# Another fixed order of two streams' steps on four engines, in a two-stream transformer decoder

## The chip, the cores and the metric

The kernel runs on one core of one Trainium2 chip. A core has four compute engines that run their own instruction lists and meet only through semaphores: TensorE (PE; its weight loads are shown as PEld), ScalarE (ACT), VectorE (DVE) and GpSimd (POOL). SyncE (SP) issues the DMA transfers. The metric is the device time of one execution in microseconds (us); the median of several is compared.

## The reference

Input `x` and context `ctx` are 32 sequences of 64 tokens with 128 channels, float32. Six sub-layers follow one another; after each one, x becomes layernorm(x + sub-layer(x)). They are:

```
x = LN(x + causal self-attention with rope(x))           16 heads of 8
x = LN(x + cross-attention(x, ctx), per-head layer norm of q and k)
x = LN(x + FP4-quantised gated FFN(x))                   inner width 352
x = LN(x + linear-attention block with convolutions and MLP(x))
x = LN(x + causal cross-attention(x, ctx))
x = LN(x + mixture of 8 experts, top 2(x))               inner width 256
```

All 8 experts are computed for every token, and weighted with the router's top-2 shares.

## The kernel before

**Streams and passes.** A chunk is 512 tokens (8 sequences, 4 tiles of 128 tokens). Two chunks are worked on at once, as two streams, called A and B here; each has its own SBUF buffers and its own 4 of the 8 PSUM banks. Two passes of a loop cover the four chunks. Both passes run the same instructions. A pass ends when all four engines are through; SP then clears the semaphores and opens the next one.

**Who does what.** On each engine a generator `network(h)` yields between steps. A step is a wait or two and then one to some thirty instructions. `weave` interleaves the steps of both streams by a list written out by hand, so many steps of A, then so many of B, and so on:

```
def weave(first, second, order):
    turns = (first, second)
    for k, count in enumerate(order):
        for _ in range(count):
            next(turns[k % 2], None)
```

`ORDER` has one list for each of the four engines. An engine executes its list strictly in this order: a step whose semaphore isn't there holds everything behind it, of both streams. Within one stream the order of steps is that of the generators.

**The steps of an attention tile t** (three attention stages, 4 tiles each), with the short names that are used below:

- S (PE, L504, in the causal stages after the mask matmuls of L497): scores. S of tile t waits for Z of tile t-1, since there is one pair of score banks per stream.
- X (DVE, L1134): row maximum; Z (DVE, L1139): subtract it. E (ACT, L913): exp.
- T (PE, L485), twice per tile: turn one half of the probabilities. ACT copies each half out of the one bank that all of them use (C, L893), so each T waits for the C of the T before it.
- M (PE, L548): probabilities times values. R (DVE, L1149 and L1152): divide. H (PE, L535): turn the heads; ACT copies them (L904 or L906). P (PE, L516): output projection. H and P of a tile share bank 3 with M, so they wait for each other's readers.
- U (DVE, L1104): add the residual, then bn_stats (L1107) and bn_aggr (L1110). POOL adds eps (L1522) and takes the power -0.5 (L1525). N (DVE, L1115): normalise. U of a tile waits for N of the tile two before.

**Between the self- and the cross-attention** each stream normalises k and then q by head on DVE (L1204 to L1234: a sum, a mean, a difference; ACT squares, L876; a second sum, L1215; then three Newton steps of three small instructions, L1190 to L1196, and a product, L1234). PE turns the result (L573), ACT applies the gain (L883) and spreads q or two of four k copies (L863, L870); POOL spreads the other two (L1553) and adds the bias to the residual (L1542). PE computes A's q (L559) and its values (L471), and ACT copies the values (L853).

**The experts' stage.** For each of 16 halves g(n) (PE, L803, gate and up matmuls) goes to ACT's silu (L1037), then DVE's product h(n) (L1469); g(n) waits for h(n-1). For each of 8 experts o(e) (PE, L794) goes to four additions on DVE (L1461); o(e) waits for h(2e+1). Ahead of it stand the router (L782), the shares (DVE, L1419 to L1452), their turning (L810) and the bias product (L816).

## Time and profile before

| what | value |
|---|---|
| median of 3 runs | 825.92 us (825.36 to 827.03) |
| the profiled execution | 826.34 us |
| its span, first to last instruction | 824.5 us |
| around the span | 1.84 us |
| mean granted TensorE clock | 0.866 |
| instructions | 13333 |

The first pass's work on PE, ACT, DVE and POOL starts at 8.6 us and ends at 415.6 us of the span; the second starts at 417.4 us and ends at 821.8 us. The second repeats the first at a distance of about 406.3 us, so the readings below are of the first pass, and each difference counts twice. A granted clock of 1.00 is 2.4 GHz, one of 0.50 is 1.2 GHz.

### The profile page before, as it was taken

How to read it: one execution, taken by the hardware profiler on the slowest of the kernel's cores; microseconds unless marked ns; L12 is line 12 of the kernel's file. 1: busy time of each engine (PE TensorE's matmuls, PEld its weight loads, DVE VectorE, ACT ScalarE, POOL GpSimd, SP SyncE). 2: the span in 40 equal slices, each digit the busy share in tenths (PEclk: the TensorE clock that was granted, in tenths of full speed). 3: DMA queues.
4: the chain of work that ended last, by engine and by line, in shares of the span. 5: the costliest groups of instructions: out<-in, count | busy, mean ns of one | idle time of the engine just before them, and what ended most of it. 6: DMA issues, size and time to landing. Idle time of an engine off the chain costs nothing.

```text
span 824.5 us, 13333 instructions
## 1 busy us (share of the span) xinstructions
PE 651.3 (79%) x5090; PEld 428.0 (52%) x5090; DVE 558.4 (68%) x1482; ACT 334.7 (41%) x546; POOL 136.7 (17%) x258
## 2 busy tenths in 40 slices
PE   5886587666796987999878756967678969789995
PEld 3565456443553554566555644654345436546663
DVE  7868576897676744655648775788967667555445
ACT  2753363223845543222146443632156546332220
POOL 3313102111025020000131240020110430100002
PEclk9997577696999888999979965976869989789998
DMA  8101000000000000000000000000000000000000
GB/s 296 51 2 52 1 2 1 1 0 2 1 0 1 2 2 0 1 1 1 2 28 2 2 0 1 2 1 1 0 2 1 1 0 3 1 1 0 1 1 26
DMA packets 9011, 10.11 MB, mean 12 GB/s; under 512 B 1256, under 2 KB 7792, under 8 KB 8560
## 3 DMA queue, kind: packets, MB, share of 16 engines
q1 hardware_dynamic: 8944, 9.22, 3.4%
q8 instruction: 42, 0.69, 0.3%
q14 instruction: 25, 0.20, 0.1%
HBM read 8.17 MB, written 1.05 MB: 11 GB/s over the span
## 4 chain that ended last, share of the span: by engine, by line
PE 55%; DVE 26%; ACT 10%; issue 4%; POOL 3%; DMA 1%; SPq 1%; POOLq 0%; DVEq 0%; ACTq 0%
PE ps L803 14%; PE ps L794 7%; PE ps L485 5%; PE ps L504 5%; PE ps L548 3%; ACT s_probs L913 3%; DVE s_probs L1139 3%; DVE s_row_max L1134 3%; PE ps L471 2%; POOL s_rs L1525 2%; DVE s_x L1115 1%; DVE s_r L1104 1%; DVE s_st L1107 1%; PE ps L516 1%; DVE s_work L1080 1%
## 5 line engine op out<-in xcount | busy, mean ns | idle before, releaser
L1522 POOL TENSOR_TENSOR s_rs<-s_mv,eps 128x1 f32<-128x1 f32 x96 | 18.9, 199 | 547.7 <-DVE s_mv L1110 368.8
L1037 ACT ACTIVATE s_k<-ps,eb 128x512 f32<-128x512 f32 x64 | 44.0, 687 | 132.9 <-PE ps L803 132.8
L1469 DVE SCALAR_TENSOR_TENSOR s_pT<-ps,eb,s_k 128x512 f32<-128x512 f32 x64 | 48.0, 750 | 60.3 <-ACT s_k L1037 57.0
L1134 DVE TENSOR_REDUCE s_row_max<-ps 128x16 f32<-128x1024 f32 x48 | 58.6, 1222 | 40.9 <-PE ps L504 40.8
L485 PE MATMUL ps<-tabs,s_probs 128*128 128x128 f32 x384 | 67.2, 303 | 18.0 <-ACT s_probs L913 15.9
L893 ACT ACTIVATE s_pT<-ps 128x512 f32<-128x512 f32 x96 | 56.8, 594 | 46.1 <-PE ps L485 45.5
L803 PE MATMUL ps<-s_xT,wg 128*128 128x512 f32 x128 | 71.3, 641 | 1.5 <-DVE s_pT L1469 1.1
L794 PEld LDWEIGHTS ps<-wo,s_pT 128*128 128x128 f32 x512 | 61.7, 192 | 17.7 <-issue 12.4
L803 PE MATMUL ps<-s_xT,wu 128*128 128x512 f32 x128 | 68.5, 618 | 0.0
L504 PE MATMUL ps<-s_k,s_q 64*64 64x256 f32 x768 | 60.6, 439 | 9.2 <-ACT s_q L863 9.2
L485 PEld LDWEIGHTS ps<-tabs,s_probs 128*128 128x128 f32 x384 | 44.5, 150 | 41.3 <-ACT s_probs L913 24.8
L794 PE MATMUL ps<-wo,s_pT 128*128 128x128 f32 x512 | 63.0, 276 | 3.1 <-DVE s_pT L1469 3.1
L913 ACT ACTIVATE s_probs<-s_probs 128x1024 f32<-128x1024 f32 x48 | 50.4, 1053 | 26.8 <-DVE s_probs L1139 26.4
L1139 DVE TENSOR_TENSOR s_probs<-ps,s_row_max 128x1024 f32<-128x1024 f32 x48 | 58.7, 1223 | 1.5
L548 PEld LDWEIGHTS ps<-s_v,s_pT 128*64 128x64 f32 x1536 | 51.1, 144 | 12.2 <-issue 12.0
L548 PE MATMUL ps<-s_v,s_pT 128*64 128x18 f32 x1536 | 55.0, 216 | 2.3 <-ACT s_headsT L904 1.9
L1525 POOL TENSOR_TENSOR s_rs<-s_rs,minus_half 128x1 f32<-128x1 f32 x96 | 52.8, 551 | 7.2
L1553 POOL TENSOR_SCALAR s_k<-s_kT,tabs 128x512 f32<-128x512 f32 x24 | 38.3, 1607 | 44.6 <-DVE s_kT L1168 22.4
L1461 DVE SCALAR_TENSOR_TENSOR s_k<-ps,s_ew,s_k 128x128 f32<-128x128 f32 x128 | 36.0, 344 | 12.3 <-PE ps L794 12.3
L504 PEld LDWEIGHTS ps<-s_k,s_q 64*64 64x64 f32 x768 | 30.5, 153 | 25.4 <-ACT s_q L863 10.8
L803 PEld LDWEIGHTS ps<-s_xT,wu 128*128 128x128 f32 x128 | 25.9, 202 | 33.4 <-issue 33.4
L516 PE MATMUL ps<-mats,s_headsT 128*128 128x128 f32 x96 | 23.9, 339 | 15.8 <-DVE s_heads L1152 13.1
(223 smaller groups left out, 1157.3 us busy)
## 6 DMA issues: line engine op xcount, KB each, us to landing
s_cin<-in_ctx SPq DMA_DIRECT2D x4, 256.0 KB, 4.7
s_xin<-in_x SPq DMA_DIRECT2D x4, 256.0 KB, 5.1
wg<-in_wg SPq DMA_DIRECT2D x1, 1024.0 KB
wu<-in_wu SPq DMA_DIRECT2D x1, 1024.0 KB
wo<-in_wo SPq DMA_DIRECT2D x1, 1024.0 KB
out_x<-s_x SPq DMA_DIRECT2D x4, 256.0 KB, 2.5
mats<-in_mats SPq DMA_DIRECT2D x1, 832.0 KB, 6.4
fc<-in_fc SPq DMA_DIRECT2D x2, 256.0 KB, 5.5
```

What stands on the lines that cost most here:

```text
L485: ins = pe.transpose(h.ps[:, 2, tile(j)], h.probs[:, t % 2, 8 * part + 2 * j:8 * part + 2 * j + 2, :] .rearrange("p h k -> p (h k)"), ident)
L504: ins = pe.matmul(h.ps[S * b:S * b + S, half, 256 * side:256 * side + 256], h.q4[rows, side, S * sq:S * sq + S], h.k4[rows, sq, :, :].rear ...
L548: ins = pe.matmul(h.ps[S * b:S * b + S, 3, 18 * j:18 * j + 18], h.pT[:, t % 2, j, S * b:S * b + S], h.v2[:, 2 * t + b, 2 * j:2 * j + 2, :] ...
L794: ins = pe.matmul(h.ps[:, 2, tile(t)], h.ehid[:, e % 2, m, tile(t)], wo[:, 2 * e + m, :], start=m == 0, stop=m == 1)
L803: ins = pe.matmul(h.ps[:, k, 0:TOK], w[:, n // 2, P * (n % 2):P * (n % 2) + P], h.xT[:, :], start=True, stop=True)
L893: act.activation(h.pT[:, t % 2, 4 * part:4 * part + 4, :].rearrange("p j q -> p (j q)"), h.ps[:, 2, :], ACT.Copy).then_inc(h.pT_here, 1)
L913: act.activation(h.probs[:, u % 2, :, :], h.probs[:, u % 2, :, :], ACT.Exp).then_inc(h.exped, 1)
L1037: act.activation(h.esg[:, n % 2, :], h.ps[:, 0, 0:TOK], ACT.Silu, bias=eb[:, 0, n:n + 1]).then_inc(h.e_silu, 1)
L1134: dve.tensor_reduce(h.row_max[:, t % 2, :], s3, AX, ALU.max).then_inc(h.max_here, 1)
L1139: dve.tensor_tensor(h.probs[:, t % 2, :, :], s3, h.row_max[:, t % 2, :].rearrange("p (h o) -> p h o", o=1).to_broadcast([P, H, S]), ALU.su ...
L1469: dve.scalar_tensor_tensor(h.ehid[:, (n // 2) % 2, n % 2, :], h.ps[:, 1, 0:TOK], eb[:, 1, n:n + 1], h.esg[:, n % 2, :], ALU.add, ALU.mult) ...
L1525: pool.tensor_tensor(h.rs[:, t % 2:t % 2 + 1], h.rs[:, t % 2:t % 2 + 1], minus_half[:, 0:1], ALU.pow).then_inc(h.rstd_here, 1)
```

## The change

Only the order changes. The four lists of `ORDER` are replaced. Two places where the generators pause are changed too: `sum_norm` no longer pauses ahead of its wait on `x_new`, and `linear_block` pauses once per tile ahead of `sum_norm`. These two move no instruction within a stream; they change what one count in DVE's list means, and DVE has 614 steps where it had 642. The instructions, their operands and their waits are the same in number and kind.

```
 ORDER = {
     "pe": (
-        3, 3, 1, 1, 1, 1, 1, 1, 3, 3, 4, 2, 5, 2, 3, 1, 2, 1, 1, 2, 1, 1, 3, 4, 1, 1, 1, 4, 2, 3, 1, 2, 1,
...
+        1, 1, 2, 2, 1, 1, 2, 2, 3, 2, 1, 1, 2, 3, 2, 1, 4, 2, 3, 1, 2, 1, 1, 1, 5, 7, 1, 2, 2, 2, 1, 3, 1,
...
     "act": (
-        1, 1, 2, 2, 2, 1, 1, 2, 2, 1, 1, 1, 1, 1, 1, 1, 2, 1, 4, 2, 2, 1, 1, 2, 1, 4, 2, 1, 2, 2, 3, 3, 2,
...
+        3, 3, 3, 3, 2, 1, 1, 1, 2, 2, 1, 1, 2, 2, 3, 1, 1, 1, 2, 2, 3, 4, 3, 2, 2, 2, 2, 3, 3, 2, 2, 1, 1,
...
     "dve": (
-        1, 1, 4, 4, 2, 2, 2, 2, 4, 2, 4, 1, 2, 1, 7, 4, 3, 1, 4, 1, 1, 1, 3, 1, 1, 1, 5, 1, 2, 1, 4, 1, 3,
...
+        1, 1, 4, 4, 2, 2, 2, 2, 2, 1, 2, 3, 6, 2, 4, 2, 10, 1, 4, 1, 3, 1, 1, 2, 3, 1, 1, 2, 1, 1, 7, 3, 1,
...
     "pool": (
-        1, 1, 1, 1, 4, 1, 2, 2, 2, 1, 2, 6, 4, 2, 4, 6, 6, 2, 2, 2, 2, 6, 3, 2, 4, 1, 5, 9, 4, 2, 4, 6, 8,
-        8,),
+        1, 1, 1, 1, 4, 2, 1, 1, 4, 6, 1, 1, 8, 8, 4, 1, 4, 3, 2, 6, 2, 2, 10, 10, 5, 1, 3, 7, 4, 3, 1, 1,
+        1, 1, 1, 2, 1, 1,),
 }
@@ -1099,7 +1099,6 @@
                 n = sub * TILES + t + 1
                 if n >= 3:
-                    yield
                     dve.wait_ge(h.x_new, n - 2)
@@ -1386,6 +1385,7 @@
                     if u < TILES:
+                        yield
                         yield from sum_norm(h, 3, u, h.ps[:, 1, tile(u)], h.x[:, u, :])
```

Written out step by step, the two orders are alike in outline: in both, the streams go through the six stages almost in step, B a little behind A. They differ in the fine order within the stages. PE's steps in the self-attention (V: values, KQ: k of the next stage, QT: L573; the first digit of T is the tile, the second the half):

```
before AV BV AS0 BS0 AT0.0 AS1 AT0.1 BT0.0 BS1 BT0.1 AT1.0 AS2 AT1.1 AM0 BT1.0 BS2 AT2.0 AS3 AH0 AT2.1 AM1
       BT1.1 BM0 AP0 AT3.0 AH1 BT2.0 AT3.1 AM2 BS3 AP1 BH0 BT2.1 AH2 BM1 AM3 AKQ AP2 BP0 BT3.0 BH1 BT3.1 AH3
       BM2 AP3 BP1 BH2 BM3 BKQ AQT BP2 BH3 BP3 BQT
after  AV AS0 BV BS0 AT0.0 AS1 AT0.1 BT0.0 BS1 AT1.0 BT0.1 AS2 AT1.1 BT1.0 BS2 BT1.1 AM0 AT2.0 BM0 AS3 AH0
       AT2.1 AM1 BT2.0 BS3 AP0 AT3.0 AH1 BH0 AT3.1 AM2 BT2.1 AP1 BM1 AH2 AM3 AKQ AP2 AH3 BP0 BT3.0 BH1 BT3.1
       BM2 BP1 BH2 AP3 BM3 BKQ AQT BP2 BH3 BP3 BQT
```

In the causal cross-attention, from S2 of B on:

```
before BS2 AT2.0 AS3 AH0 AT2.1 AM1 BT1.1 BM0 AP0 AT3.0 AH1 BT2.0 AT3.1 AM2 BS3 AP1 BH0 AH2 BT2.1 BM1 AM3 ...
after  BS2 BT1.1 BM0 AT2.0 AS3 AH0 AT2.1 BT2.0 AM1 BS3 BH0 AP0 AT3.0 AH1 AT3.1 AM2 BT2.1 AP1 BM1 AH2 AM3 ...
```

At the start and the end of the experts' stage (r router, ew turned shares, bm bias product, tx x turned):

```
before Ag0 BM3 BP2 Ag1 BH3 BP3 Btx Aew Ag2 Br Bg0 Abm Ao0 Ag3 ... Bg11 Ag14 Ao6 Bg12 Ag15 Bo5 Bg13 Ao7 Bg14 Bo6 Bg15 Bo7
after  Ag0 BM3 BP2 BH3 BP3 Ag1 Btx Br Bg0 Aew Ag2 Abm Ao0 Ag3 ... Bg11 Ag14 Bg12 Bo5 Bg13 Ao6 Bg14 Ag15 Bo6 Bg15 Ao7 Bo7
```

Of the other engines these moves are spoken of below. ACT, at the start: before, B's q (L863) stands ahead of A's values (L853); after, A's values come first. DVE, self-attention: X3 and Z3 of B stand behind A's N0 before, and ahead of A's first bn_aggr after; R0 of B stands behind A's X3 and Z3 before, and ahead of them after. DVE, per-head norms: the second sum of A's q (L1215) stands behind B's last Newton steps and L1234 before, and ahead of B's last five Newton instructions, its U3, N2 and L1234 after. ACT, same place: B's L883 and L870 for k stand ahead of A's L883 for q in both, B's take of x behind it after. POOL: the power of B's tile 1 stands behind A's L1553 after, ahead of it before; A's L1542 stands behind B's tiles 2 and 3 and B's L1553 after, ahead of them before; in the linear block B's L1553 is moved behind A's norms and L1542. DVE and ACT, entry of the causal cross-attention: B's q (L1396) is moved between A's X0 and Z0, and ACT's spreading of it (L863) ahead of A's E0. DVE, FFN: A's last two tiles come up to 9 instructions later, B's up to 8 earlier. POOL and DVE, end of the pass: the final norms of A and B, one after the other before, alternate.

## Rows read from the trace of the kernel before

**Rows 1.** The page, part 1: busy time by engine, its share, instructions.

```profile
PE 651.3 (79%) x5090; PEld 428.0 (52%) x5090; DVE 558.4 (68%) x1482; ACT 334.7 (41%) x546; POOL 136.7 (17%) x258
```

**Rows 2.** Stretches of pass 1: length; busy us of PE, PEld, DVE, ACT, POOL; clock.

```profile
26.00:57.00 31.00, 26.57 (x424) 18.58 (x415) 23.55 (x34) 18.57 (x32) 3.69 (x6) 1.00 0.01 2
...
86.00:119.00 33.00, 24.73 (x240) 16.34 (x238) 19.89 (x31) 15.03 (x24) 0.53 (x1) 0.66 0.00 1
...
147.00:200.00 53.00, 33.01 (x128) 22.30 (x128) 46.71 (x149) 12.32 (x23) 8.71 (x21) 0.76 0.00 1
...
305.00:330.00 25.00, 20.80 (x103) 12.29 (x104) 10.94 (x54) 8.86 (x13) 2.24 (x6) 0.77 0.00 0
330.00:407.00 77.00, 75.72 (x349) 47.29 (x347) 43.79 (x131) 19.61 (x29) 2.54 (x8) 1.00 0.00 1
```

**Rows 3.** Timeline, self-attention, DVE: start, us; idle time before. B's X0, A's X3, B's X3.

```profile
29.77 1.23 DVE L1134 TENSOR_REDUCE s_row_max<-ps 128x16 f32<-128x1024 f32 x1 [0.25 <-PE ps L504]
...
43.99 1.21 DVE L1134 TENSOR_REDUCE s_row_max<-ps 128x16 f32<-128x1024 f32 x1
...
53.94 1.22 DVE L1134 TENSOR_REDUCE s_row_max<-ps 128x16 f32<-128x1024 f32 x1
```

**Rows 4.** Timeline, self- to cross-attention, ACT.

```profile
24.14 1.34 ACT L853 ACTIVATE s_v<-ps 64x256 f32<-64x256 f32 x4
...
77.90 1.36 ACT L853 ACTIVATE s_v<-ps 64x256 f32<-64x256 f32 x4 [4.82 <-PE ps L471]
79.28 0.63 ACT L876 ACTIVATE s_probs<-s_probs 128x512 f32<-128x512 f32 x1
```

**Rows 5.** Timeline, self- to cross-attention, POOL.

```profile
70.64 3.11 POOL L1553 TENSOR_SCALAR s_k<-s_kT,tabs 128x512 f32<-128x512 f32 x2 [3.85 <-ACT s_kT L883]
```

**Rows 6.** Timeline, self- to cross-attention, DVE.

```profile
73.83 1.20 DVE L1222 TENSOR_SCALAR s_work<-s_work 128x64 int32<-128x64 int32 x1
...
80.27 0.68 DVE L1215 TENSOR_REDUCE s_work<-s_probs 128x64 f32<-128x512 f32 x1
```

**Rows 7.** Timeline, first scores of the cross-attention, PE.

```profile
88.87 1.98 PE L504 MATMUL ps<-s_k,s_q 64*64 64x256 f32 x16 [2.29 <-ACT s_q L863]
```

**Rows 8.** Timeline, last norm of the FFN stage, DVE.

```profile
198.73 0.35 DVE L1115 TENSOR_SCALAR s_x<-s_r,s_mv,s_rs 128x128 f32<-128x128 f32 x1 [0.71 <-POOL s_rs L1525]
```

**Rows 9.** Timeline, entry of the causal cross-attention, ACT.

```profile
263.72 1.28 ACT L913 ACT_TABLE_LOAD   x1
```

**Rows 10.** Timeline, causal cross-attention, PE: M0 and S3 of B.

```profile
286.48 1.11 PE L548 MATMUL ps<-s_v,s_pT 128*64 128x18 f32 x32
...
291.54 1.03 PE L504 MATMUL ps<-s_k,s_q 64*64 64x256 f32 x16
```

**Rows 11.** Timeline, causal cross-attention, DVE: B's q; X3 of B; N3 of A.

```profile
264.99 0.74 DVE L1396 TENSOR_SCALAR s_qT<-ps,cols 128x512 f32<-128x512 f32 x1
...
294.01 1.22 DVE L1134 TENSOR_REDUCE s_row_max<-ps 128x16 f32<-128x1024 f32 x1
...
303.14 0.35 DVE L1115 TENSOR_SCALAR s_x<-s_r,s_mv,s_rs 128x128 f32<-128x128 f32 x1 [0.71 <-POOL s_rs L1525]
```

**Rows 12.** Timeline, start of the experts, PE: g1 of A, bias product, g5 of A.

```profile
312.68 1.58 PE L803 MATMUL ps<-s_xT,wg 128*128 128x512 f32 x2
...
326.94 1.15 PE L816 MATMUL ps<-bout,s_k 8*128 8x128 f32 x8
...
337.90 1.12 PE L803 MATMUL ps<-s_xT,wg 128*128 128x512 f32 x2 [0.56 <-DVE s_pT L1469]
```

**Rows 13.** Timeline, end of the pass, PE: o7 of B.

```profile
407.94 2.05 PE L794 MATMUL ps<-wo,s_pT 128*128 128x128 f32 x16 [1.56 <-DVE s_pT L1469]
```

**Rows 14.** Timeline, end of the pass, POOL: first and last norm of B.

```profile
411.65 0.19 POOL L1522 TENSOR_TENSOR s_rs<-s_mv,eps 128x1 f32<-128x1 f32 x1 [4.26 <-DVE s_mv L1493]
...
414.66 0.55 POOL L1525 TENSOR_TENSOR s_rs<-s_rs,minus_half 128x1 f32<-128x1 f32 x1
```

**Rows 15.** Timeline, end of the pass, DVE: last norm of B.

```profile
415.24 0.34 DVE L1115 TENSOR_SCALAR s_x<-s_k,s_mv,s_rs 128x128 f32<-128x128 f32 x1 [0.49 <-POOL s_rs L1525]
```

More of the change, by code:

```diff
@@ L93 @@
     "pe": (
[5 rows of a table removed]
-    "act": (
[5 rows of a table removed]
-    "dve": (
[8 rows of a table removed]
[5 rows of a table added]
+    "act": (
[4 rows of a table added]
+    "dve": (
[9 rows of a table added]
     "pool": (
-        1, 1, 1, 1, 4, 1, 2, 2, 2, 1, 2, 6, 4, 2, 4, 6, 6, 2, 2, 2, 2, 6, 3, 2, 4, 1, 5, 9, 4, 2, 4, 6, 8,
-        8,),
+        1, 1, 1, 1, 4, 2, 1, 1, 4, 6, 1, 1, 8, 8, 4, 1, 4, 3, 2, 6, 2, 2, 10, 10, 5, 1, 3, 7, 4, 3, 1, 1,
+        1, 1, 1, 2, 1, 1,),
 }
@@ L1101, in sum_norm @@
                 if n >= 3:
-                    yield
                     dve.wait_ge(h.x_new, n - 2)
@@ L1388, in linear_block @@
                     if u < TILES:
+                        yield
                         yield from sum_norm(h, 3, u, h.ps[:, 1, tile(u)], h.x[:, u, :])
```

36 rows, old and new, of the table ORDER are left out of this document.

## The prediction

> **What bounds the kernel now.** I read the page first. PE is busy for 79% of the span and DVE for 68% [rows 1], so neither is full, and an order can gain only where both wait. The change adds, removes and resizes nothing, so its price is all in waits. I therefore read the stretches next, for who is full where [rows 2]. From 330 to 407 us PE is busy for 75.72 of 77 us at the upper clock level (2.4 GHz): the experts can't shrink, only start earlier or end without holes. From 147 to 200 us DVE is busy for 46.71 of 53 us: the FFN's quantising is DVE's, and reordering can win a few us at most. In the attention stages nobody is full: in 26 to 57 us PE has 26.57 of 31 us and DVE 23.55. There the chain runs round DVE, ACT and PE, and each hole in DVE ahead of a row maximum shows in the timeline. These stages and their seams are where the fine order matters. The second pass repeats the first, so each difference counts twice.
>
> I then followed the new order of all four engines, stage by stage, with the durations of the timeline, and wrote down each time at which a step can start: the later of its data and of the step ahead of it on its engine. Six differences come out. Each is in us of one pass.
>
> **1. Self-attention and the seam behind it: +2.0.** The start moves one step. A's values are copied by ACT (1.34 us for the four parts [rows 4]) ahead of B's q, and A's first scores no longer wait for B's values on PE. That gives A 0.3 us, but B's copy chain starts 1.34 us later, and with it X0 of B (29.77 us, 0.25 us of idle time ahead of it [rows 3]) comes at 31.3 us: DVE idles. DVE's order makes A's next maximum wait for B's Z0, so A is late by 1.1 us from there. With 1.23 us for each X and Z [rows 3] DVE does X and Z of A1 from 33.7 us, of B1 from 36.9 us and of A2 from 39.3 us to 41.75 us. Then PE does BT1.0, BS2, BT1.1, AM0, AT2.0 and BM0 ahead of AS3: BT1.1 ends at 42.9 us, AM0 (1.11 us, as in [rows 10]) at 44.0, AT2.0 at 44.6, BM0 at 45.6, AS3 at 46.8. X3 of A moves from 43.99 us to 46.9 us, and X3 of B, which PE and DVE now take earlier, from 53.94 us to 51.5 us [rows 3]. What is late next is A's tail: its tiles' bn_aggr stands behind B's X3 and Z3, and its last products, QT and k are 1.8 us late. ACT's copy of A's values comes at 79.05 us instead of 77.90 us, and behind it stands the square (0.63 us) [rows 4] for which A's second sum waits (80.27 us [rows 6]). In the new order DVE does that sum ahead of B's last Newton steps, so DVE stands idle for about 1.8 us with B's work queued behind. POOL adds to it: B's second power stands behind A's spreading of k (3.11 us [rows 5]), so B's N1 comes at 76 us. In return the residual's addition is moved away, and the 1.20 us that a 64-column instruction took beside it falls back to about 0.2 us [rows 6]. The first scores of the cross-attention (88.87 us [rows 7]) come out between 90.4 and 91.3 us by this walk; with all of POOL's and DVE's waits in full it is +3.1, with half the holes filled by small instructions +1.0. I take +2.0.
>
> **2. Cross-attention, FFN and linear block: +0.3.** In the cross-attention A's tail is put ahead of B's: A reaches the quantising 1.3 us earlier and B ends it 2 us later. In the FFN this is given back, since DVE is nearly full and B's third tile moves ahead of A's last: A's norm is 2.2 us late, but B's last norm, which ends the stage (198.73 us [rows 8]), is late by only 0.3 us. The linear block keeps that: its swaps (A's second rope ahead of B's projections, A's x ahead of B's elu) meet again at B's kv product. POOL's k copies behind A's norms free A's x by 2 us, but PE is busy with B's MLP until then. The ends are wide, -1.5 to +2.0, because DVE's 149 instructions of that stretch [rows 2] are reshuffled.
>
> **3. Entry of the causal cross-attention: -0.3.** B's q (264.99 us [rows 11]) now goes ahead of A's Z0, and ACT spreads it ahead of A's E0, so B's first scores start 0.4 us earlier and A's E0 2 us later, just when PE has ended them. The load of exp's table (1.28 us [rows 9]), which was hidden ahead of A's exp, now follows B's spreading and eats what is left. Ends: 0 and -0.5.
>
> **4. Causal cross-attention: -1.8.** BT1.1 and BM0 go ahead of AT2.0 and AS3 (1.1 us late for A, the length of BM0 [rows 10]), but BS3 moves up from 291.54 us [rows 10] to about 287.5 us. X3 of B then fills a hole of DVE: it starts at 288.9 us where it stood at 294.01 us [rows 11]. So B's eighth of the maxima no longer stands between A's last tiles, and A's N3, at 303.14 us before [rows 11], ends the stage 1.85 us earlier. The walk loses 1.0 us of it if B's M1 and A's P1 collide, and could gain 0.4 more: -0.8 to -2.2.
>
> **5. Start of the experts: -1.7.** B's last H and P go ahead of A's g1, so g1 (312.68 us [rows 12]) starts 1.5 us late, but B's x is ready 3.6 us earlier. PE had idle time there: 20.80 us busy of 25 us, at a granted clock of 0.77 [rows 2]. The bias product, at 326.94 us before [rows 12], comes 1.2 us earlier if the same work takes as long, and the 0.56 us ahead of g5 (337.90 us [rows 12]) goes too, as its h is moved ahead of B's eight share instructions. From there PE is full and carries the gain to the end of the stage. Ends: +0.5 (PE at the lower level throughout) and -2.5 (at the upper).
>
> **6. End of the pass: -0.9.** PE waits 1.56 us for h15 of B ahead of the last o7 of B [rows 13]. With Ao7 put between, PE ends 2.05 us earlier. But A's eight additions and norms, done 8 us earlier before, now fall together with B's. POOL had four norms from 411.65 us to the end of the last power at 415.21 us [rows 14], with DVE's last norm at 415.24 us [rows 15]; now eight norms of two POOL instructions each alternate, six of them after 409.6 us at some 0.77 us each (0.19 and 0.55 us [rows 14] and the latency). The last one ends at 414.3 us, DVE's N at 414.7 us. Ends: -0.4 and -1.6.
>
> **The sum.** 2.0 + 0.3 - 0.3 - 1.8 - 1.7 - 0.9 = -2.4 us a pass, -4.8 us in both. The profiled execution took 826.34 us (824.5 us of span and 1.84 us around it), so its like would take 821.5 us. The median of the runs lies 0.42 us below that execution: 821.1 us. The half-widths of the six terms (1.05, 1.75, 0.25, 0.7, 1.5, 0.6) add up as independent errors to 2.7 us a pass. Both passes have the same order, hence 5.4 us for both, 815.7 to 826.5 us for this case alone. A difference under 0.2%, 1.65 us, couldn't be told from no change.
>
> **Rival 1, slower: PE's clock falls in the self-attention.** Now the stretch runs at 1.00, while the cross-attention, with the same steps and more holes, was granted 0.66 [rows 2], and its scores took 1.98 us [rows 7] against 1.03 us at the upper level [rows 10]. The new order adds 2 to 3 us of holes between 27 and 47 us. If a third of PE's 26.57 us there ran at the lower level, it would take 8.9 us more, and about half lies on the path: +4.4 a pass, which makes +2.0 a pass and 829.9 us. It decides from +3.2 a pass on. For it speaks how close the two stretches are in kind; against it, that PE is still busy for most of the stretch. The Trainium skill (TensorE: Matmul & The Clock Gate, Part 1: The HAM clock gate) says that the slow clock is the default and that activity releases it; by that rule a thinner PE stretch risks the clock and a denser one keeps it, and this trace agrees as far as 1.00 beside 26.57 of 31 us and 0.66 beside 24.73 of 33 us show it. Chance 0.20.
>
> **Rival 2, no change.** The gains of term 4 and 5 are A's and B's ends at the seam to the experts. If B's h0 there, with silu's table load before it, holds the first full experts back, term 5 is worth 0 and term 4 half: 2.0 + 0.3 - 0.3 - 0.9 - 0.9 = +0.2 a pass, 826.3 us. For it: DVE idled before most of these steps already, so PE may have slack that I count as path. Chance 0.19.
>
> **Rival 3, faster than the sum: the clock returns earlier before the experts.** 20.80 us of PE work at a mean of 0.77 [rows 2] would take 16 us at 1.00. If the denser order there brings half of it, 2.0 us a pass beyond the sum, the time is 817.1 us. Chance 0.13. The sum's own case keeps 0.48.
>
> **Range and chances.** 815.5 to 828.0 us leaves out most of rival 1 and the far ends of the others, about 2 in 10. The sum's case lies under 824.3 us nearly always (0.45 of its 0.48; 0.02 within the bound, 0.01 above), rival 2 gives 0.16 within it and 0.01 faster and 0.02 slower, rival 1 all but slower (0.19, and 0.01 no change), rival 3 faster. Faster 0.59, same 0.19, slower 0.22.
>
> **What the profile after would show.** Term 1: a hole of 1.5 to 2 us ahead of DVE's second row maximum, A's X3 at 46.9 us, B's at 51.5 us, the cross-attention's first scores at 90 to 91.5 us. Term 2: the last norm of the FFN 2 to 2.5 us later than before. Term 4: B's X3 five us earlier against A's X0, and N3 of A at about 303.2 us, its old time, with the loss of term 1 made good. Term 5: no wait ahead of g5. Term 6: no wait ahead of B's o7, and norms of both streams alternating. The prediction is wrong if the first scores of the cross-attention come at their old time or after 92 us, if the clock of 26 to 57 us falls below 0.9, or if the bias product doesn't come 3 us earlier against the entry of the causal cross-attention.

## The result, and the profile after

| | median | runs |
|---|---|---|
| before | 825.64 us | 4 (823.81 to 827.03) |
| changed | 819.33 us | 4 (819.11 to 819.74) |
| ratio | 0.9919 | 95% interval 0.9900 to 0.9938 |

The new order is 6.3 us faster. Forecast were 821.1 us and 815.5 to 828.0 us. The profiled execution took 819.74 us, its span 817.9 us, with a mean granted clock of 0.874.

Part 1 of the page shows that the work is the same ([rows 1] is its counterpart): DVE's busy time falls by 10.5 us with the same 1482 instructions, PE's by 1.6 us. By the traces the single durations of these 1482 add up to 618.0 us before and 613.2 us now; the rest of the 10.5 us is that more of them overlap. 2.0 us of these 4.8 are one 64-column instruction in each pass (L1222, now L1221) that took 1.20 us beside POOL's addition [rows 6] and takes 0.20 us now, as the prediction said.

```profile
PE 649.7 (79%) x5090; PEld 429.9 (53%) x5090; DVE 547.9 (67%) x1482; ACT 333.5 (41%) x546; POOL 138.4 (17%) x258
```

The same stretches of pass 1 as in [rows 2]; the last one ends at 404 us instead of 407, since PE is done earlier. The last numbers of a row are the granted clock, the DMA share and GB/s. The clock of 26 to 57 us is still 1.00, so rival 1 did not come true there.

```profile
26.00:57.00 31.00, 26.44 (x415) 18.60 (x416) 22.18 (x28) 20.74 (x34) 3.79 (x4) 1.00 0.01 2
...
147.00:200.00 53.00, 35.94 (x141) 23.65 (x138) 47.72 (x155) 11.61 (x23) 9.85 (x23) 0.73 0.00 1
305.00:330.00 25.00, 22.04 (x105) 12.57 (x106) 12.28 (x60) 8.94 (x14) 2.34 (x6) 0.81 0.00 0
330.00:404.00 74.00, 73.97 (x352) 47.33 (x351) 40.00 (x114) 19.05 (x29) 0.00 (x0) 1.00 0.00 1
```

DVE's timeline in the self-attention, the counterpart of [rows 3]: B's X0, A's X3, B's X3. A's S0 comes 0.58 us later than before in this pass, because the first loads do. Less that, the three stand at 31.7, 47.3 and 51.8 us; the forecast was 31.3, 46.9 and 51.5. The hole ahead of the first is 2.16 us.

```profile
32.27 1.23 DVE L1133 TENSOR_REDUCE s_row_max<-ps 128x16 f32<-128x1024 f32 x1 [2.16 <-PE ps L504]
...
47.86 1.23 DVE L1133 TENSOR_REDUCE s_row_max<-ps 128x16 f32<-128x1024 f32 x1 [0.65 <-PE ps L504]
...
52.40 1.21 DVE L1133 TENSOR_REDUCE s_row_max<-ps 128x16 f32<-128x1024 f32 x1
```

PE's timeline right behind that: A's M3 and KQ, A's H3, B's M2, B's KQ, and the first scores of the cross-attention, the counterpart of [rows 7]. M3 takes 1.50 us, where such a product takes 1.11 us at the upper clock level [rows 10]. PE then waits 1.60 us ahead of A's H3 (L1103 is U, A's third sum), and B's P0 stands behind it. The first scores come at 94.79 us, 5.92 us later than before, where 90.4 to 91.3 us were forecast and "after 92 us" was named ahead as one of the signs that the prediction is wrong.

```profile
57.74 1.50 PE L548 MATMUL ps<-s_v,s_pT 128*64 128x18 f32 x32 [0.41 <-issue]
59.17 2.08 PE L559 MATMUL ps<-mats,s_cT 128*128 128x128 f32 x8
...
63.28 0.30 PE L535 MATMUL ps<-tabs,s_heads 128*128 128x128 f32 x1 [1.60 <-DVE s_r L1103]
...
66.10 1.90 PE L548 MATMUL ps<-s_v,s_pT 128*64 128x18 f32 x32
...
72.70 2.08 PE L559 MATMUL ps<-mats,s_cT 128*128 128x128 f32 x8
...
94.79 1.09 PE L504 MATMUL ps<-s_k,s_q 64*64 64x256 f32 x16 [2.62 <-ACT s_q L863]
```

DVE's timeline: the last norm of the FFN (counterpart of [rows 8]), 1.36 us later than before and no longer 5.9; then A's X0, B's X3 and A's N3 of the causal cross-attention (counterpart of [rows 11]). From A's X0 to B's X3 are 25.95 us; before they were 31.41 (294.01 [rows 11] less 262.60 for X0). A's N3 was forecast at about 303.2 us.

```profile
200.09 0.35 DVE L1114 TENSOR_SCALAR s_x<-s_r,s_mv,s_rs 128x128 f32<-128x128 f32 x1 [0.71 <-POOL s_rs L1525]
...
263.52 1.22 DVE L1133 TENSOR_REDUCE s_row_max<-ps 128x16 f32<-128x1024 f32 x1
...
289.47 1.23 DVE L1133 TENSOR_REDUCE s_row_max<-ps 128x16 f32<-128x1024 f32 x1 [0.39 <-PE ps L504]
...
302.79 0.35 DVE L1114 TENSOR_SCALAR s_x<-s_r,s_mv,s_rs 128x128 f32<-128x128 f32 x1
```

PE's timeline, counterpart of [rows 12, 13]: A's g1 1.5 us late, the bias product 2.4 us early, g5 3.3 us early and with no wait ahead of it; Ao7 and Bo7, which are now one run of 32 matmuls with no wait. Against the first matmul of the causal cross-attention the bias product comes 3.7 us earlier in pass 1 and 2.8 us in pass 2; the prediction had named 3 us.

```profile
314.20 1.85 PE L803 MATMUL ps<-s_xT,wg 128*128 128x512 f32 x2
...
324.53 1.15 PE L816 MATMUL ps<-bout,s_k 8*128 8x128 f32 x8
...
334.56 1.07 PE L803 MATMUL ps<-s_xT,wg 128*128 128x512 f32 x2
...
401.17 3.78 PE L794 MATMUL ps<-wo,s_pT 128*128 128x128 f32 x32
```

DVE's last norms, counterpart of [rows 15]: A's and B's alternate, and the last starts at 411.19 us instead of 415.24.

```profile
410.68 0.35 DVE L1114 TENSOR_SCALAR s_x<-s_k,s_mv,s_rs 128x128 f32<-128x128 f32 x1 [0.46 <-POOL s_rs L1525]
411.19 0.35 DVE L1114 TENSOR_SCALAR s_x<-s_k,s_mv,s_rs 128x128 f32<-128x128 f32 x1 [0.17 <-POOL s_rs L1525]
```

**Where the time went, by stage.** Below, a pass is cut at instructions that both kernels have, and each length is the difference of two starts. The rows are the stretches of pass 1 by the trace. Before: A's S0 to A's turned q (L573; the new order has 31 more matmuls in it, one product of B); B's first cross-attention scores to the linear block's L683; A's S0 of the causal cross-attention to the router's product; from there to g5 of A; from there to the last norm of B.

```profile
25.63:68.61 42.98, 35.17 (x516) 25.96 (x516) 32.58 (x72) 21.76 (x38) 6.86 (x14) 0.95 0.05 14
105.98:199.40 93.42, 67.20 (x569) 48.03 (x570) 76.80 (x222) 30.04 (x54) 13.66 (x34) 0.77 0.00 1
260.19:305.17 44.98, 35.67 (x478) 23.65 (x478) 30.07 (x60) 22.85 (x35) 6.47 (x15) 0.90 0.01 2
305.17:337.90 32.73, 27.91 (x130) 15.99 (x129) 17.70 (x88) 10.92 (x16) 2.24 (x6) 0.82 0.00 1
337.90:415.24 77.34, 70.49 (x336) 45.28 (x336) 41.65 (x114) 17.64 (x26) 5.86 (x16) 0.98 0.00 1
```

The same five of the changed kernel:

```profile
26.21:74.57 48.36, 40.26 (x547) 30.58 (x548) 33.19 (x71) 23.20 (x40) 6.68 (x13) 0.87 0.04 9
110.75:200.76 90.01, 66.70 (x570) 45.61 (x570) 76.00 (x222) 29.80 (x54) 14.39 (x34) 0.80 0.00 1
261.44:304.46 43.02, 36.22 (x477) 24.70 (x478) 29.08 (x57) 23.66 (x37) 6.21 (x15) 0.88 0.01 2
304.46:334.56 30.10, 27.14 (x131) 15.95 (x130) 16.09 (x81) 10.90 (x17) 2.34 (x6) 0.84 0.00 1
334.56:411.19 76.63, 70.36 (x338) 45.24 (x336) 42.35 (x122) 17.56 (x26) 5.57 (x16) 0.99 0.01 1
```

All stages of both passes, in us (before / changed; "entry" is from A's first turned x to A's S0):

| stage | pass 1 | pass 2 | forecast |
|---|---|---|---|
| entry | 16.15 / 16.09 | 14.09 / 12.97 | not priced |
| A's S0 to B's first cross-attention scores | 80.35 / 84.53 | 80.16 / 83.02 | +2.0 |
| from there to L683 of the linear block | 93.42 / 90.01 | 92.20 / 92.09 | +0.3 |
| to A's causal S0 | 60.79 / 60.68 | 61.74 / 61.64 | -0.3 |
| to A's router product | 44.97 / 43.02 | 44.90 / 43.13 | -1.8 |
| to g5 of A | 32.74 / 30.09 | 32.72 / 30.71 | -1.7 |
| to the last norm of B | 77.34 / 76.64 | 77.34 / 76.63 | -0.9 |
| sum | 405.76 / 401.07 | 403.15 / 400.19 | -2.4 |

Passes gained 4.7 and 3.0 us where 2.4 were forecast for each; about 1 us of it is lost outside of the passes, since the first loads land 0.6 us later and the end behind the last norm is 0.4 us longer. The second half of a pass went as forecast. In the first half two terms missed in opposite directions: the self-attention and its seam cost 4.2 and 2.9 us instead of 2.0, and cross-attention with FFN gave back 3.4 us in pass 1, where +0.3 was forecast.

### The profile page after: what moved, and what is told of

Read it like the earlier page. It is cut to its first block, busy times and chain, and to the rows that moved or that the text cites. A ratio compares the mean times of both kernels' runs of the same rounds, so it can differ in the third digit from the quotient of the medians.

```text
span 817.9 us, 13337 instructions
## 1 busy us (share of the span) xinstructions
PE 649.7 (79%) x5090; PEld 429.9 (53%) x5090; DVE 547.9 (67%) x1482; ACT 333.5 (41%) x546; POOL 138.4 (17%) x258
## 4 chain that ended last, share of the span: by engine, by line
PE 61%; DVE 21%; ACT 10%; issue 5%; POOL 2%; DMA 1%; SPq 1%; POOLq 0%; DVEq 0%; ACTq 0%
PE ps L803 14%; PE ps L794 7%; PE ps L548 6%; PE ps L504 6%; PE ps L485 5%; PE ps L471 3%; PE ps L516 2%; PE ps L559 2%; PE ps L747 2%; PE ps L752 2%; DVE s_r L1103 1%; ACT s_v L853 1%; ACT s_probs L913 1%; DVE s_row_max L1133 1%; DVE s_probs L1138 1%
## 5 line engine op out<-in xcount | busy, mean ns | idle before, releaser
L1522 POOL TENSOR_TENSOR s_rs<-s_mv,eps 128x1 f32<-128x1 f32 x96 | 20.8, 219 | 527.0 <-DVE s_mv L1109 349.0
L485 PE MATMUL ps<-tabs,s_probs 128*128 128x128 f32 x384 | 67.4, 306 | 20.1 <-ACT s_probs L913 16.2
L548 PEld LDWEIGHTS ps<-s_v,s_pT 128*64 128x64 f32 x1536 | 54.8, 151 | 14.8 <-issue 13.9
L548 PE MATMUL ps<-s_v,s_pT 128*64 128x18 f32 x1536 | 59.2, 221 | 3.7 <-issue 2.7
L1553 POOL TENSOR_SCALAR s_k<-s_kT,tabs 128x512 f32<-128x512 f32 x24 | 37.6, 1580 | 35.2 <-DVE s_kT L1167 21.4
L650 PE MATMUL ps<-gu_w,s_xT 128*128 128x352 f32 x64 | 29.3, 592 | 4.2 <-DVE s_hq L1271 3.5
```

Of the source, the lines that this page charges most:

```text
L485: ins = pe.transpose(h.ps[:, 2, tile(j)], h.probs[:, t % 2, 8 * part + 2 * j:8 * part + 2 * j + 2, :] .rearrange("p h k -> p (h k)"), ident)
L548: ins = pe.matmul(h.ps[S * b:S * b + S, 3, 18 * j:18 * j + 18], h.pT[:, t % 2, j, S * b:S * b + S], h.v2[:, 2 * t + b, 2 * j:2 * j + 2, :] ...
```

## The experiments

The first eleven kernels are the kernel before or the changed kernel with another order in part of a pass; the twelfth is the changed kernel again. They run the same steps. Both pauses of the generators are kept in each (`yield` ahead of the wait on `x_new`, and ahead of `sum_norm` in the linear block), so that both orders can be written in one set of lists. A list is cut where both orders have taken the same steps of A and of B on that engine:

| cut: steps of A, of B | PE | ACT | DVE | POOL |
|---|---|---|---|---|
| k, behind A's KQ and P2 of the self-attention | 28, 18 | 21, 17 | 29, 17 | 6, 2 |
| s, start of the seam | 30, 27 | 23, 21 | 56, 29 | 11, 6 |
| x, ahead of the cross-attention's scores | 33, 30 | 28, 25 | 70, 56 | 12, 12 |
| f, start of the FFN | 59, 57 | 48, 46 | 147, 129 | 20, 20 |
| c, start of the causal cross-attention | 95, 85 | 77, 75 | 238, 224 | 42, 42 |
| e, start of the experts | 123, 119 | 94, 91 | 275, 259 | 50, 50 |

The diffs below give each engine's list by these cuts, `old[x:c]` being the old order from cut x to cut c. What such a join looks like in the list of PE (the kernel with only the new row maxima, against the one with the whole first part old):

```
     "pe": (
-        3, 3, 1, 1, 1, 1, 1, 1, 3, 3, 4, 2, 5, 2, 3, 1, 2, 1, 1, 2, 1, 1, 3, 4, 1, 1, 1, 4, 2, 3, 1, 2, 1, 1,
+        3, 3, 1, 1, 2, 2, 3, 2, 1, 1, 2, 3, 2, 1, 4, 2, 3, 1, 2, 1, 1, 1, 4, 4, 1, 1, 1, 4, 2, 3, 1, 2, 1, 1,
...
```

Three batches of four ran, each on one chip. The kernel before had medians of 829.76, 827.33 and 828.86 us in them, so ratios to it are compared. Only one profile of it exists, of an execution of 826.34 us. Lengths of stages are compared with that one, which is up to 3.4 us shorter than a batch's median, so a ratio and the lengths beside it need not add up.

### Halves and quarters of a pass

**Only the first part new.**

```
-order = old
+order = new[:x] + old[x:]
```

> Only the first part of a pass has the new order (self-attention and the seam, up to the first cross-attention scores); from there on the old order. Recorded terms: +2.0 us per pass, so 825.6 + 4.0 = 829.6. Rival A (the trace of the changed kernel shows the first cross-attention scores 5.1 us late in pass 1 and 3.4 in pass 2, and the new order of cross-attention is what gives it back): +8, so 833 to 834. Rival B (the lateness is slack that any order of the middle takes up): under +1, so 826.

Ratio 1.0031 (1.0014 to 1.0047), or +2.6 us. That is nearer to the recorded terms (1.0048) and to rival B (1.0012) than to rival A (1.0097), and the interval leaves out all three, the first two narrowly. The trace shows why one number is too simple: pass 1 took 411.82 us (+6.1), pass 2 403.14 us (no loss). From A's S0 to A's turned q it took this in pass 1 (the new order has 547 matmuls in the stretch, as in the changed kernel), and 45.34 us in pass 2:

```profile
25.13:75.39 50.26, 42.09 (x548) 31.68 (x549) 33.56 (x72) 22.52 (x39) 6.96 (x13) 0.81 0.03 10
```

**Only the middle new.**

```
-order = old
+order = old[:x] + new[x:c] + old[c:]
```

> Only cross-attention, FFN and linear block have the new order. Recorded terms: +0.3 - 0.3 = 0 per pass, so 825.6. Rival A (the new order of the middle is itself worth the 4.2 and 0.9 us that were given back there in the two passes): -5, so 820.5. Rival B: 0, so 825.6.

Ratio 0.9909 (0.9885 to 0.9934), -7.5 us: rival A's direction, and more than its size. In the profiled execution the stretch from B's first scores to L683 took 90.12 and 90.13 us, against 93.42 and 92.20 before.

```profile
106.49:196.61 90.12, 65.37 (x570) 44.99 (x570) 75.97 (x222) 29.80 (x54) 14.38 (x34) 0.82 0.00 1
256.55:303.96 47.41, 38.55 (x477) 26.05 (x478) 29.94 (x60) 24.04 (x37) 6.50 (x15) 0.81 0.01 2
```

DVE is as busy as before there (75.97 against 76.80 us) and idles 14.2 us instead of 16.6. The second row is the old causal cross-attention behind the new middle: 47.41 us, 2.4 more than behind the old middle, at a clock of 0.81 where it was 0.90. So what the new middle gains is in part lost behind it. Pass 1 of this execution is 405.9 us long, as before the change, and pass 2 is 399.7 us (3.5 us less): the profile shows some 4 us of the 7.5.

**The first half new, and the second half new.**

```
-order = old
+order = new[:c] + old[c:]
```

> The new order from the start of a pass to the start of causal cross-attention, the old one behind it. Recorded terms: +2.0 per pass, so 829.6. Both rivals, from the trace of the changed kernel (causal cross-attention entered 0.3 us early against its own entry in pass 1, 1.7 late in pass 2): +1.4, so 827.0.

```
-order = old
+order = old[:c] + new[c:]
```

> The old order up to the start of causal cross-attention, the new one behind it. Recorded terms: -1.8 - 1.7 - 0.9 = -4.4 per pass, so 816.8. From the trace of the changed kernel (-4.6 and -3.8 in the two passes): 817.2, faster than the changed kernel. Rival (what the second half gains hangs on how the new first half hands the streams over): -2 to -3 per pass, so 820 to 822.

Ratios 0.9957 (0.9939 to 0.9975) and 0.9922 (0.9897 to 0.9948), or -3.6 and -6.5 us. The first half does gain by itself, so neither the recorded +4.0 nor the rivals' +1.4 holds. The second half gains less than its terms alone (-8.8); its trace has 45.10 us from causal S0 to the router, as before the change, where the changed kernel has 43.02. The last theory (the gain hangs on the handover) comes nearest.

### Single stages, and the best join

**Only the cross-attention new.**

```
-order = old
+order = old[:x] + new[x:f] + old[f:]
```

> Only cross-attention, up to A's first FFN products, has the new order. Theory 1 (the gain of the middle, ratio 0.9909, is made in cross-attention's second half: A's blocks run ahead of B's, so TensorE has no hole there and its granted clock stays at 1.00 from 130 to 145 us, where the kernel before has 0.73 and 0.59): ratio 0.992 to 0.995. Theory 2 (it is made by the order of VectorE's steps in the FFN and the linear block): 1.000.

Ratio 1.0013 (0.9992 to 1.0034): no gain, theory 1 fell and the number is theory 2's. A's last projection of the stage does come 26.3 us behind B's first scores instead of 30.5, and the clock is 1.00 from 130 to 140 us (before: 0.73 and 0.59 in its two halves). But with the old FFN behind it the stretch to L683 still takes 92.42 us. With the new FFN behind it, the kernel with the whole middle new takes 90.12 us. So the gain needs the new FFN too, alone or with the new cross-attention; the new FFN behind the old cross-attention was not run. The experts' start then took 34.63 us (32.74 before), at a clock of 0.71.

**The old first part, all else new.**

```
-order = new
+order = old[:x] + new[x:]
```

> The old order in self-attention and the seam, the new one from the first cross-attention scores on. Theory 1 (the parts add: the middle's 0.9909 and the second half's 0.9922): ratio 0.983. Theory 2 (they don't, since what one part gains meets a bound in the next; the changed kernel, 0.9919, without the 0.3% that its first part costs alone): 0.989. Recorded terms (+2.0 us per pass taken away): 0.987.

Ratio 0.9698 (0.9672 to 0.9723), a median of 804.17 us: better than either kernel, and beyond the sum of the parts (0.983, theory 1), as neither theory had it. Three stretches of its pass 1 (self-attention, causal cross-attention, experts' start):

```profile
26.21:69.18 42.97, 35.16 (x516) 25.94 (x516) 32.58 (x72) 21.77 (x38) 6.87 (x14) 0.94 0.05 14
...
257.04:300.09 43.05, 36.23 (x478) 24.69 (x478) 29.05 (x56) 23.63 (x37) 6.21 (x15) 0.88 0.01 2
300.09:330.19 30.10, 27.15 (x131) 15.98 (x130) 16.11 (x81) 10.89 (x17) 2.34 (x6) 0.84 0.00 1
```

Against the changed kernel's first profile, its passes are 4.8 and 10.2 us shorter (396.24 and 390.02). In pass 1 all of it is made before cut x; in pass 2 only 4 us are, and the rest comes in each later stage but the last.

**Only the causal cross-attention new.**

```
-order = old
+order = old[:c] + new[c:e] + old[e:]
```

> Only causal cross-attention has the new order. Recorded term: -1.8 us per pass, ratio 0.9956. Rival, from the run with the new order in the second half (its router scores stand 0.85 us after the old place, where the causal cross-attention was entered 0.72 late, though B's last scores are 3.4 us earlier): nothing is gained by itself, 1.000.

Ratio 1.0045 (1.0020 to 1.0069): slower, which no theory had. Both stretches behind cut c:

```profile
260.60:305.72 45.12, 39.19 (x477) 26.56 (x478) 29.38 (x59) 22.71 (x35) 6.27 (x15) 0.78 0.01 2
305.72:340.83 35.11, 30.75 (x131) 17.81 (x130) 17.84 (x88) 10.93 (x16) 2.25 (x6) 0.70 0.00 1
```

B's S3 comes 27.3 us behind A's S0 as planned (31.4 before), but the stage is no shorter. The same 477 matmuls were busy for 39.19 us at a clock of 0.78, against 35.67 us at 0.90 before, and the experts' first products run slow as well (30.75 us at 0.70 against 27.91 at 0.82). So the same matmuls keep PE busy for 3.5 and 2.8 us longer at the lower clock. The twelve executions show the same: ten took 830.1 to 834.5 us at mean clocks of 0.839 to 0.850, and two took 824.33 and 826.24 us at 0.868 and 0.866, a little less than the kernel before (827.33 us). So in its executions with the higher clock this order does not lose.

**Only the experts new.**

```
-order = old
+order = old[:e] + new[e:]
```

> Only the experts have the new order. Recorded terms: -1.7 at their start and -0.9 at the end of the pass, -5.2 us in all, ratio 0.9937. Rival (the start's gain needs B's earlier end of causal cross-attention, whose last block holds B's router scores back): the end of the pass alone, -0.9 per pass, 0.9978.

Ratio 0.9887 (0.9863 to 0.9910), -9.3 us: the recorded -5.2 is too small, and the rival (the end alone) fell. The start of the experts gains without the new causal order:

```profile
306.88:335.83 28.95, 25.97 (x131) 15.65 (x130) 16.09 (x81) 10.71 (x16) 2.33 (x6) 0.86 0.00 1
```

28.95 and 29.01 us, -3.8 and -3.7 a pass; the end is 76.62 us in both, -0.72.

### What in the new first part costs

**The new row maxima alone** (the new order up to A's P2).

```
-order = new
+order = new[:k] + old[k:x] + new[x:]
```

> The changed kernel with the new order of self-attention only up to A's query-key products of the last step (so with the new order of the row maxima); A's fourth turn of heads, the rest of self-attention and the seam are old, everything behind them new. The new first part as a whole costs 0.9919 against 0.9698, about 9 us per pass. Recorded step (the later row maxima of A carry the loss): 0.985 to 0.992. Rival 1 (the loss is made behind them, by A's fourth turn of heads ahead of B's third projection): 0.970 to 0.973. Rival 2 (the clock: it falls as soon as the row maxima move, at 57 us and not at 63, and half speed costs 1 us for each us of TensorE's work): 0.975 to 0.980.

**The fourth turn of heads alone.** PE takes A's H3 ahead of B's P0, T3.0, H1 and T3.1; ACT's copy and square of A and DVE's sums of A move with it, since the lists must agree.

```
-order = new
+order = old[:k] + new[k:s] + old[s:x] + new[x:]
```

> The changed kernel with the old row maxima (self-attention's first part), then the new order from A's fourth turn of heads ahead of B's third projection to the end of self-attention, then the old seam and the new rest. Recorded step: 0.970, since nothing there was priced. Rival 1 (TensorE stood 1.60 us idle ahead of that turn in the changed kernel, with B's projection, turns and sums of heads behind it, and B's query-key products 6.0 late where A's last row maximum was 3.9): +2 to +3 us per pass, 0.975 to 0.977.

**The seam alone.**

```
-order = new
+order = old[:s] + new[s:]
```

> The changed kernel with the old self-attention, and the new order only in the seam (B's last norms and its query and key chain beside the start of A's cross-attention), and behind it. Recorded term (part of +2.0, under 1 us per pass): 0.971 to 0.972. Rival (B's turned queries were 8.9 us late in the changed kernel where A's were 6.0; that is the seam's own loss of 3 us, but B's scores were only 4.8 late): 0.970.

**The changed kernel again.**

It has no edit.

> The changed kernel as it is, beside the three above on one chip. If its ratio belongs to the order and not to one chip: 0.990 to 0.994. If the sum of the parts decides (with the old first part 0.9698), the three above must share its distance to 0.9698.

| kernel | ratio | interval | A's S0 to turned q, passes 1 and 2 | A's S0 to B's first cross-attention scores | clock falls, us behind A's S0 | span of its profile |
|---|---|---|---|---|---|---|
| old first part | 0.9698 | 0.9672 to 0.9723 | 42.97, 42.97 | 80.1, 79.0 | 38, 37 | 803.4 |
| new row maxima | 0.9766 | 0.9723 to 0.9809 | 44.03, 44.41 | 79.8, 81.4 | 41, 40 | 801.2 |
| new fourth turn | 0.9820 | 0.9783 to 0.9856 | 45.67, 45.67 | 84.3, 83.2 | 33, 33 | 813.9 |
| new seam | 0.9722 | 0.9686 to 0.9758 | 44.39, 42.95 | 79.9, 79.2 | 39, 37 | 807.4 |
| all new | 0.9850 | 0.9806 to 0.9895 | 45.34, 47.04 | 80.0, 82.6 | 41, 37 | 804.3 |

The old first part is from the batch ahead. The profiled execution is not the middle one of a kernel: with the new row maxima and with all new it was the fastest of six (803.05 and 806.18 us, medians 807.76 and 816.55), with the new seam the slowest (809.17, median 805.85). The sixth column is when the granted clock left 1.00 at the end of the self-attention.

**The fourth turn costs the most.** By ratio it is 1.2% over the old first part, where its rival had expected 0.5 to 0.7%, and B's first scores come 4 us later in both passes. In its profile PE waits 1.29 us ahead of A's H3, and the changed kernel waits there for 1.60 or 1.80 us in every pass; with the new row maxima alone it is 0.19 us, with the old order 0.04 us. So the wait is the order's. Behind it the clock falls at 33 us instead of 37 or 38. Both rows have the same 516 matmuls, busy for 37.61 us here and 35.16 us with the old first part: 2.45 of the 2.70 us by which the stretch is longer is PE's work at the lower level, and PE's idle time grew by 0.25 us only.

```profile
58.94 0.45 PE L535 MATMUL ps<-tabs,s_heads 128*128 128x128 f32 x1 [1.29 <-DVE s_r L1103]
```

**The row maxima cost less, and by how much is open.** Their stretch is 1.1 and 1.4 us longer, but it holds 31 more matmuls, one product of B, which takes 1.11 us at the upper level [rows 10]. B's first scores come 0.4 us earlier in pass 1 and 2.4 us later in pass 2. The ratio lies in the band that rival 2 had given (0.975 to 0.980), though its mechanism isn't seen.

**The parts do not simply add.** In pass 2 of all new the stretch is 4.1 us longer than the old one, the sum of both parts. In its pass 1, and in pass 2 of the kernel with only the first part new, the clock fell at 41 us and the stretch took 45.34 us: 2.4 us over the old one, and 1.3 us over the new row maxima alone, whose clock fell at 41 us too. So where the clock stays the turn costs about 1.3 us up to A's turned q. The same order took 47.04 to 47.06 us in the three passes in which the clock fell at 37 us, and 48.36, 49.48 and 50.26 us where it fell at 31 to 34 us (in the last one it was low at the start too).

Stretches of pass 1, new row maxima first, new turn second:

```profile
24.23:68.25 44.02, 36.41 (x547) 27.28 (x548) 32.98 (x73) 22.80 (x40) 7.41 (x14) 0.97 0.05 14
```

```profile
25.29:70.97 45.68, 37.61 (x516) 28.10 (x517) 33.08 (x71) 21.87 (x38) 6.40 (x13) 0.86 0.04 10
```

Rival 2, in which the clock falls as soon as the row maxima move, is not seen: that execution kept 1.00 up to 65 us, longer than the kernel before (0.90 from 60 to 65 us). The clock came with the turn (0.83 from 55 to 60 us, 0.50 from 60 to 70). The seam's run can't decide between its two expectations (0.971 to 0.972, and 0.970): the interval holds both. The intervals also overlap for the old first part against the new seam (0.9698 and 0.9722), the latter against the new row maxima (0.9766), and the new turn against all new (0.9820 and 0.9850).

**One kernel, two executions.** The last run is the changed kernel without any edit, and its six executions took 806.18, 810.67, 815.19, 817.91, 818.41 and 818.83 us, at mean clocks of 0.893, 0.889, 0.877, 0.874, 0.876 and 0.871. The four of the first measurement had taken 819.1 to 819.7 at 0.874. So the ratio is 0.9850 here and 0.9919 there, and the expectation that it belongs to the order alone (0.990 to 0.994) fell; chip and execution are not told apart by this. The profiled execution is the fastest, with a span of 804.3 us. Four stages of its pass 1, to be read beside the changed kernel's first four rows above:

```profile
24.23:69.57 45.34, 36.86 (x548) 27.66 (x549) 33.59 (x72) 22.87 (x40) 6.95 (x13) 0.96 0.05 13
104.22:194.38 90.16, 65.40 (x569) 45.04 (x570) 75.94 (x222) 29.80 (x54) 14.35 (x34) 0.82 0.00 1
254.67:296.82 42.15, 35.22 (x477) 23.45 (x478) 28.95 (x57) 23.51 (x37) 6.20 (x15) 0.92 0.01 2
296.82:325.46 28.64, 25.66 (x131) 14.84 (x130) 16.09 (x81) 10.92 (x17) 2.33 (x6) 0.88 0.00 1
```

The first stretch lasts 45.34 us instead of 48.36, with PE busy for 36.86 us at 0.96 instead of 40.26 at 0.87; the fourth 28.64 instead of 30.10. The work is the same instruction by instruction, and DVE's busy time agrees within 0.4 us. At the place where the two part, the kernel before, the changed kernel's first execution, then this one:

```profile
55.00:60.00 5.00, 3.74 (x46) 3.11 (x42) 4.59 (x14) 1.82 (x3) 0.00 (x0) 1.00 0.00 0
60.00:65.00 5.00, 2.63 (x41) 1.91 (x41) 3.80 (x19) 1.56 (x4) 1.40 (x4) 0.90 0.01 2
```

```profile
55.00:60.00 5.00, 4.32 (x74) 3.75 (x73) 2.39 (x10) 1.82 (x3) 1.51 (x4) 0.83 0.01 3
60.00:65.00 5.00, 3.00 (x16) 2.33 (x15) 3.17 (x9) 1.38 (x4) 0.00 (x0) 0.83 0.01 2
```

```profile
55.00:60.00 5.00, 2.79 (x48) 2.43 (x44) 3.62 (x12) 0.28 (x1) 0.75 (x2) 1.00 0.00 0
60.00:65.00 5.00, 3.42 (x46) 2.63 (x46) 3.97 (x19) 2.08 (x5) 0.90 (x3) 1.00 0.01 2
65.00:70.00 5.00, 4.66 (x46) 4.48 (x47) 3.61 (x16) 0.28 (x1) 1.44 (x4) 0.57 0.37 108
```

In one execution of the changed kernel the clock left 1.00 between 55 and 60 us, in the other after 65 us. The order being the same, this goes with 3 us in this stage; what made the clock fall earlier in one is not shown. A's KQ, which took 2.08 us in the first, in the second:

```profile
56.79 1.16 PE L559 MATMUL ps<-mats,s_cT 128*128 128x128 f32 x8
```

## Why the prediction was right

It was right in sign and size (819.33 us where 821.1 us were forecast). Point by point it was right in the second half of a pass and wrong by compensating amounts in the first, so that the sum came so near is in part luck. One of the three signs that it had named for being wrong came true: the first scores of the cross-attention came after 92 us, at 94.79. The other two did not: the clock of 26 to 57 us stayed at 1.00, and the bias product came 3.7 and 2.8 us earlier where 3 were named.

**Term 1, +2.0 (1.0 to 3.1): mis-sized.** Measured from A's S0 to B's first cross-attention scores: +4.2 and +2.9 us a pass, and -0.3 and +2.4 in the second profile of the same kernel (79.99 and 82.60 us). Two of the four lie outside of the range. The walk round DVE was right to within 0.4 us up to B's X3. What failed is the sentence behind it, that A's last products, QT and k are 1.8 us late: QT came 5.4 us later against A's S0 in the first profile, 4.1 in its pass 2, and 2.4 in pass 1 of the second profile. The sentence left out a step that PE's new list shows plainly, A's H3 ahead of B's P0, T3.0, H1 and T3.1, and what is queued behind it. H3 waits for DVE's third sum of A, which DVE takes behind three instructions on KQ's result. PE stood still for 1.60 us in the profile above; the run with that part alone has +2.7 us in both passes up to A's turned q, of which 2.45 us are longer PE work, and a pass in which the clock stays has +1.3. The forecast also took every PE duration as before, but from 58 us on the clock was lower: M3 took 1.50 us, and KQ 2.08 where the second profile's ran in 1.16.

**Term 2, +0.3 (-1.5 to +2.0): wrong sign.** The stretch from B's first scores to L683 is 3.4 us shorter in pass 1 and 0.1 us in pass 2; in both passes of the second profile and of the kernel with the new middle alone it is 90.0 to 90.2 us, 2.1 to 3.3 us less than before. Over all kernels with the new middle it took 90.0 to 90.3 us in eleven passes of sixteen and 91.1 to 92.5 us in five, over those with the old one 92.2 us in three passes of ten and 93.4 us in seven. The step that failed is that A's lead from the cross-attention "is given back" in the FFN. With the old FFN it is (92.42 us); with the new one DVE idles 14.0 us instead of 16.6 in that stretch of pass 1. In pass 2 of the first profile it idled 16.2 us, where it had idled 15.4 before, and why that pass kept nothing is open. I had counted the delay of single norms there, not DVE's idle time, though DVE was the engine that I had named as nearly full.

**Term 3, -0.3:** -0.1 in both passes. **Term 4, -1.8:** -1.95 and -1.8. B's X3 moved as said, and A's N3 stands at 302.79 us. But the experiments show that the gain is not this stage's own: the new causal order behind the old middle gains nothing (45.12 us against 44.98), and the old one behind the new middle loses 2.4 us. In both, PE's clock was 0.78 to 0.81 instead of 0.88 to 0.92. The term was right for a kernel in which both halves change.

**Term 5, -1.7 (+0.5 to -2.5):** -2.65 and -2.0; up to -4.1 in the second profile and -3.8 with only the experts new. The ends of the range, which were called "PE at the lower level throughout" and "at the upper", were the right thing to watch: with the new order this stretch took, among others, 28.6, 30.1 and 31.1 us at clocks of 0.88, 0.84 and 0.77, with DVE busy for 16.1 us each time. The far end was too near: -4.1 lies outside of -2.5.

**Term 6, -0.9:** -0.70 and -0.71, and 76.60 to 76.64 us in every pass of every kernel with the new end, against 77.33 to 77.35 with the old. PE ends earlier and the norms alternate as forecast.

**Not priced:** the entry of pass 2, 14.09 us before and 12.97 changed. It is worth about 1 us once. Its cause is open: kernels with the old end had 12.70 to 14.29 us there, those with the new end 12.72 to 14.57.

**The rivals.** Rival 1's mechanism exists, at another place than was named. The clock of 26 to 57 us stayed 1.00, but it fell right behind that stretch, some 6 us earlier than before (0.83 from 55 to 60 us, where the kernel before had 1.00 there and 0.90 from 60 to 65), and went with some 3 us of that stage in the first profile. Rival 2 fell: the experts' start gains by itself. Rival 3 came true in one pass at most: 305 to 330 us ran at 0.81 instead of 0.77, and from the router's product to g5 the clock was 0.84 instead of 0.82 in pass 1 but 0.78 instead of 0.83 in pass 2. The Trainium skill (TensorE: Matmul & The Clock Gate, Part 1: The HAM clock gate) was quoted ahead for activity releasing the fast clock. The kernel with only the causal cross-attention new shows that a busy PE is not enough of a sign: its stretch from 300 to 325 us ran at 0.50 throughout with PE busy for 20.79 of 25 us, the same stretch before at 0.73 with 18.60 us busy:

```profile
300.00:325.00 25.00, 20.79 (x109) 12.75 (x108) 10.98 (x57) 6.41 (x12) 4.41 (x12) 0.50 0.00 1
```

Busy time is itself longer at the lower level, so it can't be read as activity. Why the clock stayed down in that kernel and came back in others is open. No run here held the order fixed and changed PE's activity alone; only the two executions of one kernel separate the clock from the order.

**What decides the total** is therefore shown only in part. The parts do not add: the middle is worth -7.5 us and the second half -6.5 us by themselves, the experts -9.3, and all of it with the old first part -25 us. Where a stage has the same order and the same matmuls in two kernels, its length follows the granted clock (the old causal cross-attention took 44.98 us at 0.90 and 47.41 at 0.81, the new one 43.02 at 0.88 and 45.12 at 0.78). So the clock goes with much of the difference; by what rule it moves is not shown.

## What to carry to other kernels

When a written order changes on several engines, walk it step by step on each engine and, for every step that is moved ahead, ask what it waits for and what then stands behind it; the one such step that I passed over cost 1.3 us a pass up to A's turned q where the clock stayed and 2.7 us where it fell with it, against the 2.0 us of the whole term in which it lay. Where an engine is nearly full over a stage, price the stage by that engine's idle time, not by single steps' delays. And test an order by parts before keeping it whole: here the same lists with one part put back are 1.8 to 3.0% faster than before, where the whole is 0.8 to 1.5%.

## What the runs showed of the hardware

- One program ran in 819.1 to 819.7 us in one measurement and in 806.2 to 818.8 us in another. Two of its profiled executions differ by 13.6 us of span, at mean clocks of 0.893 and 0.874, with the same work. The Trainium skill (TensorE: Matmul & The Clock Gate, Part 1: The HAM clock gate) says that the count of slow matmuls at a start varies from run to run, and puts the penalty of that start under 1% of a typical span. The clocks of the two traces here part between 55 and 65 us, well behind the start, and their spans differ by 1.7%, so that bound doesn't cover this scatter. A forecast of 1% for such a kernel is near to what executions differ by.
- PE's work takes 1.11 us for M (32 matmuls of 18 columns) and 1.16 us for KQ (8 of 128 columns) at the upper level and 1.90 and 2.08 us at the lower, as the rows above show, and a stage is longer by most of the difference: 3.0 us of length for 3.4 us of busy time in the self-attention.
- Stage lengths come in few values. The old self-attention stretch took 42.95 to 42.98 us in 13 of the 16 passes that have it, and 43.60, 44.39 and 44.43 us in three first passes. In these three the granted clock was below 1.00 for a time between 25 and 35 us already (0.83 over these 10 us in each of them), where the kernel before had 1.00.
